# Fourth layer of a graph network: two edge tiles summed in one PSUM bank, and two of three pairs of tiles gathered plainly

## Chip, cores and metric

The kernel runs on one core of a Trainium2 chip. The metric is device time in microseconds (us) of one execution of the whole program, the median of several runs. Everything is one launch.

## What is computed

A node table x of 3125 rows and 256 columns goes through four graph layers, each followed by `x = layernorm(x + layer(x))`. There are 53125 edges with a source, a destination (sorted), 128 attributes and a type. Only the fourth layer matters here. It is a transformer convolution done twice (relu between), with 4 heads of 64 channels:

```
k_j   = k[src] + e                  # e = edge_attr @ We + be
alpha = einsum('ehc,ehc->eh', q[dst], k_j) / 8
ex    = exp(alpha - segment_max(alpha, dst)[dst])
msg   = (v[src] + e) * ex / segment_sum(ex, dst)[dst]
out   = segment_sum(msg, dst) + x @ Ws + bs
```

## The kernel before

Nodes stand in 25 blocks of 128 rows. The sorted edges are cut into tiles of 128 edges, each tile with destinations in one block only: 440 tiles (`ET`), about 17 or 18 to a block. The function `attend` runs one pass over all 440 tiles; it is called twice, for the two convolutions. Two neighbouring tiles are a pair (220 pairs, `PAIRS`), eight pairs a batch of 16 tiles (`NB`).

For each pair, the engines do this:

- GpSimd gathers, with one indirect DMA a tile, 128 rows of 516 floats (key, value and a column a head) by source from `kv_tab` into `t_kv`, a ring of 40 tiles (`UB`). There are two ways. An *accumulating* gather (L1850) adds the rows to what stands in the ring; ScalarE has first filled it with the edge terms (`fill`, L1962 and L1963). A *plain* gather (L1846) writes the rows, and VectorE adds the edge terms afterwards (`add_edge_terms`, L1872 and L1874). `plain(p)` says which pair is which: before, every second one.
- TensorE makes the edge terms (L2022), and picks the queries of the destinations with one-hot matrices (`queries`, L2034).
- VectorE multiplies keys and queries (L1884), sums over channels (L1890), takes its share in the running softmax of a batch (`sm.dve`), and weighs two of four heads of eight tiles at once (L1899); ScalarE weighs the other two (L2003) and makes one-hots of destinations (L1972, L1974).
- TensorE multiplies a tile's one-hots by its weighed rows (`scatter`, L2053): the tile's sums over destinations, 128 x 260, in one of three PSUM banks (`WIN3`). VectorE adds this window to the block's sums in `acc` in SBUF (`add_window`, L1921), at a block number held in a register (loaded eight at a time, L154).

The order is written out by hand as steps. In step p each engine treats pair p in its first half of the work and pair q = p - 11 (`LAG`) in its second: the sums of pair q are multiplied in TensorE's step p and added in VectorE's step p + 1. There is one semaphore `products` (TensorE's finished tiles), which frees one-hots, ring slots and lets VectorE add, and one `added` (VectorE's additions), which frees the banks. On entering a new batch, VectorE rescales a block's sums for the new maximum (`rescale`, L1912).

Ahead of the passes, `start_up` makes the tables from the sorted edges. All phases are separated by a barrier of all engines.

## Time and profile before

| | us |
|---|---|
| median of 3 runs | 4127.81 |
| lowest, highest | 4125.18, 4128.53 |
| span of the profiled execution, first to last instruction | 4145.4 |
| pass 1: first gather to last addition to the sums | 2475.8 to 3228.9 |
| pass 2: the same | 3348.0 to 4098.7 |

The profiled execution is not timed by itself beside its span; the three runs are executions of the same program without the profiler. PE is TensorE, PEld its weight loads, DVE VectorE, ACT ScalarE, POOL GpSimd, SP SyncE; a q behind a name is that engine's instruction queue. A row's duration includes its start and its drain, so two rows of one engine can overlap by some 80 ns: what an instruction costs its engine is read from start to next start.

### The profile page before, as it was taken

How to read it: one execution, taken by the hardware profiler on the slowest of the kernel's cores; microseconds unless marked ns; L12 is line 12 of the kernel's file. 1: busy time of each engine (PE TensorE's matmuls, PEld its weight loads, DVE VectorE, ACT ScalarE, POOL GpSimd, SP SyncE). 2: the span in 40 equal slices, each digit the busy share in tenths (PEclk: the TensorE clock that was granted, in tenths of full speed). 3: DMA queues.
4: the chain of work that ended last, by engine and by line, in shares of the span. 5: the costliest groups of instructions: out<-in, count | busy, mean ns of one | idle time of the engine just before them, and what ended most of it. 6: DMA issues, size and time to landing. Idle time of an engine off the chain costs nothing. (4 is left out here: it accounts for less than half of the span.)

```text
span 4145.4 us, 56575 instructions
## 1 busy us (share of the span) xinstructions
PE 2931.3 (71%) x12389; PEld 2013.0 (49%) x12389; DVE 2921.6 (70%) x6934; ACT 1927.7 (47%) x5796; POOL 2507.2 (60%) x2316
## 2 busy tenths in 40 slices
PE   4566566266777795467666587888888878888884
PEld 3444444144444463344444335666665446666662
DVE  3455555577777754355555648999999759999997
ACT  3444444211111133222223446878787348888884
POOL 5666664366666301666666048888886268888881
PEclk7667777578888896666767799999999999999997
DMA  5655444366666421344434249999997489999993
GB/s 158 136 135 132 133 135 105 121 187 202 200 201 193 154 92 53 106 114 114 113 111 110 41 151 225 223 219 223 219 224 180 139 200 223 226 222 226 225 222 104
DMA packets 363228, 673.24 MB, mean 162 GB/s; under 512 B 65028, under 2 KB 167413, under 8 KB 362910
## 3 DMA queue, kind: packets, MB, share of 16 engines
q0 software_dynamic: 160896, 403.63, 43.2%
q1 hardware_dynamic: 197902, 262.18, 19.4%
q10 hardware_dynamic: 4112, 3.83, 0.3%
q8 instruction: 123, 2.02, 0.2%
q14 instruction: 195, 1.60, 0.1%
HBM read 579.68 MB, written 89.74 MB: 161 GB/s over the span
## 5 line engine op out<-in xcount | busy, mean ns | idle before, releaser
L1850 POOL DMA_INDIRECT t_kv<-kv_tab,srcT x440 | 713.0, 1620 | 152.7 <-issue 130.7
L2053 PE MATMUL bank<-t_kv,t_oh 128*128 128x260 f32 x1760 | 519.8, 404 | 144.6 <-DVE acc L1921 68.3
L1410 POOL DMA_INDIRECT grow<-h_tab,srcT x440 | 417.1, 948 | 297.7 <-issue 98.1
L533 POOL DMA_INDIRECT grow<-h_tab,srcT x440 | 418.0, 950 | 251.6 <-issue 110.7
L878 POOL DMA_INDIRECT grow<-x_tab,srcU x416 | 394.3, 948 | 245.7 <-issue 109.4
L1846 POOL DMA_INDIRECT t_kv<-kv_tab,srcT x440 | 456.4, 1037 | 134.1 <-issue 123.1
L1013 PE MATMUL bank<-grow,oh 128*128 128x272 f32 x832 | 324.7, 497 | 195.1 <-DVE acc L931 107.8
L2022 PE MATMUL bank<-we,t_aT 128*128 128x256 f32 x1760 | 436.4, 388 | 24.1 <-DMA t_aT<-attrT_tab 21.0
L2003 ACT ACTIVATE t_kv<-t_kv 128x64 f32<-128x64 f32 x1696 | 445.2, 333 | 0.0
L2053 PEld LDWEIGHTS bank<-t_kv,t_oh 128*128 128x128 f32 x1760 | 284.8, 191 | 261.1 <-issue 150.5
L2034 PE MATMUL bank<-H,t_ohT 128*128 x2640 | 367.5, 276 | 18.8 <-DVE t_ks L1884 18.4
L608 DVE TENSOR_TENSOR acc<-acc,bank 128x258 f32 x440 | 186.7, 424 | 271.9 <-PE bank L704 120.1
L704 PE MATMUL bank<-grow,oh 128*128 128x258 f32 x880 | 334.6, 551 | 58.5 <-DVE acc L608 40.3
L1921 DVE TENSOR_TENSOR acc<-acc,bank 128x260 f32 x880 | 366.8, 417 | 11.5 <-PE bank L2053 6.6
L1526 PE MATMUL bank<-grow,oh 128*128 128x257 f32 x880 | 348.0, 539 | 29.2 <-DVE acc L1452 24.8
L2022 PEld LDWEIGHTS bank<-we,t_aT 128*128 128x128 f32 x1760 | 332.6, 195 | 74.0 <-DMA t_aT<-attrT_tab 22.6
L1452 DVE TENSOR_TENSOR acc<-acc,bank 128x257 f32 x440 | 185.2, 421 | 246.3 <-DMA atail<-in_edge_attr 118.4
L1884 DVE TENSOR_TENSOR t_ks<-t_kv,bank 128x512 f32<-128x512 f32 x440 | 299.7, 681 | 66.0 <-DMA t_kv<-kv_tab,srcT 56.6
L931 DVE SCALAR_TENSOR_TENSOR acc<-bank,in_first,acc 128x272 f32 x416 | 208.0, 500 | 188.7 <-PE bank L1013 72.9
L966 ACT COPY H<-bank 128x512 f32<-128x512 f32 x110 | 64.2, 586 | 556.4 <-PE bank L986 232.5
L1013 PEld LDWEIGHTS bank<-grow,oh 128*128 128x128 f32 x832 | 157.8, 227 | 314.3 <-issue 306.1
L2034 PEld LDWEIGHTS bank<-H,t_ohT 128*128 128x128 bf16 x2640 | 255.6, 99 | 104.3 <-issue 26.1
(406 smaller groups left out, 5611.5 us busy)
## 6 DMA issues: line engine op xcount, KB each, us to landing
t_aT<-attrT_tab SPq DMA_DIRECT2D x110, 512.0 KB
H<-in_edge_attr SPq DMA_DIRECT2D x440, 64.0 KB
attrT_tab<-H SPq DMA_DIRECT2D x55, 512.0 KB
t_ohT<-place_tab SPq DMA_DIRECT2D x110, 256.0 KB
H<-lo_tab SPq DMA_DIRECT2D x55, 256.0 KB
grow<-h_tab,srcT POOLq DMA_INDIRECT x880
place_tab<-H SPq DMA_DIRECT2D x55, 256.0 KB
wbig<-place_tab SPq DMA_DIRECT2D x55, 256.0 KB
```

What stands on the lines that cost most here:

```text
L533: nc.gpsimd.indirect_dma_start(out=grow[:, t % RA, :], out_offset=None, in_=h_tab, in_offset=bass.IndirectOffsetOnAxis(ap=srcT[:, t:t + 1] ...
L878: nc.gpsimd.indirect_dma_start(out=grow[:, t % RA, 0:F], out_offset=None, in_=x_tab, in_offset=bass.IndirectOffsetOnAxis(ap=srcU[:, t:t + ...
L1013: nc.tensor.matmul(PS[t % WIN1][:, 0:AC], oh[:, g % 2, u, :], grow[:, t % RA, :], start=True, stop=True).then_inc(products, 1)
L1410: nc.gpsimd.indirect_dma_start(out=grow[:, t % R2, :], out_offset=None, in_=h2_tab, in_offset=bass.IndirectOffsetOnAxis(ap=srcT[:, t:t + 1 ...
L1526: nc.tensor.matmul(PS[2 + t % WIN2][:, 0:F + 1], oh[:, t // HB % 2, t % HB, :], grow[:, t % R2, 0:F + 1], start=True, stop=True).then_inc( ...
L1846: nc.gpsimd.indirect_dma_start(out=kv[:, u, :], out_offset=None, in_=kv_tab, in_offset=row).then_inc(g_ready[u], 16)
L1850: nc.gpsimd.indirect_dma_start(out=kv[:, u, :], out_offset=None, in_=kv_tab, in_offset=row, compute_op=ALU.add).then_inc(g_ready[u], 16)
L1921: nc.vector.tensor_tensor(window, window, PS[4 + t % WIN3][:, 0:LHW], ALU.add).then_inc(added, 1)
L2003: last = nc.scalar.activation(part, part, ACT.Copy, scale=u_rows[:, t % UB, h, C3:C3 + 1])
L2022: mm = nc.tensor.matmul(PS[j % 2][:, v * F:(v + 1) * F], aT[:, g % 3, u * P:(u + 1) * P], we[:, :], start=True, stop=True)
L2034: mm = nc.tensor.matmul(PS[2 + p % 2][:, v * F:(v + 1) * F], ohT[:, g % 3, u * P:(u + 1) * P], Q3[:, ds(blocks[u], 1), n, :].rearrange("p ...
L2053: nc.tensor.matmul(PS[4 + t % WIN3][:, 0:LHW], oh[:, t % OHS, :], kv[:, t % UB, F:KVW], start=True, stop=True).then_inc(products, 1)
```

## The change

Tiles of a pair are now summed in PSUM where they belong to the same block. The one-hot product of pair r's first tile opens window r in a bank. The product of its second tile is made one pair later, after the first product of pair r + 1: it adds into window r if both tiles have the same block, and into window r + 1 if a new block begins with it. A number for each pair (`turn_i`, 0 or 1), made at start-up, says which; TensorE loads it into a register and takes the bank from it. This needs at least two tiles in each block, so the tile count of a block is raised to 2 where it is lower. The last pair of each batch can't share with the next batch, since the sums are rescaled between: its second tile has a window of its own. That makes 220 + 28 = 248 windows a pass, in the same three banks. `products` counts pairs now. VectorE adds windows one step later, the steps are one more, and the rescaling is one step later. Besides, two of three pairs are gathered plainly (146 plain pairs, 74 accumulating). The eight PSUM banks are declared as one tensor; two small tensors are given free earlier to make room.

```diff
+def last_of_batch(r):
+    return r % PB == PB - 1 or r == PAIRS - 1
+def window_no(r):
+    return r // PB * (PB + 1) + r % PB
...
+        def window_by_turn(first, r, turn, width):
+            here, there = r % PB % WINS, (r % PB + 1) % WINS
+            two = BANKS[:, first + here:first + there + 1, :] if here < there else BANKS[:, first:first + WINS, :][:, ::-2, :]
+            return two[:, ds(turn, 1), 0:width].rearrange("p a c -> p (a c)")
...
+                        step(nc.vector.tensor_scalar(n_b[:, 0:NT], n_b[:, 0:NT], 2.0, None, ALU.max))
...
+                        dve.wait_ge(starts_in, 32)
+                        nc.vector.tensor_tensor(turn_i[:, :], block_i[0:1, 1:ET:2], block_i[0:1, 0:ET:2], ALU.not_equal)
...
-        STEPS = PAIRS + LAG + 1
+        STEPS = PAIRS + LAG + 2
...
-            return p % 2 == 1
+            return p % 3 > 0
...
-                                    pool.wait_ge(products, t + 2 - UB)
+                                    pool.wait_ge(products, (t - UB) // 2 + 1)
...
-                            if 1 <= q:
-                                add_window(first, blocks[first % HB])
+                            if q >= 2 and q % 4 == 2:
+                                blocks = following
+                            if q >= 2 and not last_of_batch(q - 2):
+                                add_window(q - 2, blocks)
+                            elif q >= 2:
+                                add_own_window(q - 2, blocks)
                             if p < PAIRS:
                                 sum_channels(p)
-                            if 1 <= q:
-                                add_window(first + 1, blocks[(first + 1) % HB])
-                            if q >= 0 and q % 4 == 0 and q < PAIRS:
-                                blocks = following
+                            if q >= 1 and last_of_batch(q - 1):
+                                add_window(q - 1, blocks)
...
-                            if q >= 0 and q % 8 == 0 and q < PAIRS:
-                                sm.take_factor(dve, q // 8)
-                                rescale(q // 8, blocks[0])
+                            if q % PB == 0 and 0 <= q < PAIRS:
+                                sm.take_factor(dve, q // PB)
+                            if q % PB == 1 and 0 < q < PAIRS:
+                                rescale(q // PB, following[0])
...
-                                if t >= WIN3:
-                                    pe.wait_ge(added, t - WIN3 + 1)
-                                nc.tensor.matmul(PS[4 + t % WIN3][:, 0:LHW], oh[:, t % OHS, :],
-                                                 kv[:, t % UB, F:KVW], start=True, stop=True).then_inc(products, 1)
+                        def first(r):
+                            t, n = 2 * r, window_no(r)
...
+                            if n >= WINS:
+                                pe.wait_ge(added, n - WINS + 1)
+                            nc.tensor.matmul(window_of(4, r, LHW), oh[:, t % OHS, :], kv[:, t % UB, F:KVW], start=True, stop=True, skip_group_check=True)
+
+                        def second(r, turn):
+                            t, n = 2 * r + 1, window_no(r) + 1
...
+                            if last_of_batch(r):
+                                pe.wait_ge(added, n - WINS + 1)
+                                nc.tensor.matmul(own_window_of(4, r, LHW), ones_of, rows_of, start=True, stop=True, skip_group_check=True).then_inc(products, 1)
+                            else:
+                                nc.tensor.matmul(window_by_turn(4, r, turn, LHW), ones_of, rows_of, start=False, stop=True, skip_group_check=True).then_inc(products, 1)
...
                             if 0 <= q < PAIRS:
-                                scatter(q)
+                                first(q)
+                                if q % PB:
+                                    if q % 4 == 1:
+                                        turn = turns(q - 1, 4)
+                                    second(q - 1, turn[(q - 1) % 4])
+                                if last_of_batch(q):
+                                    second(q, None)
```

## Rows read from the trace of the kernel before

**Rows 1.** Cores: span and mean granted TensorE clock.

```profile
core 0: 4145.4 us, clock 0.841
```

**Rows 2.** Windows: length, busy us (instructions) of PE, PEld, DVE, ACT, POOL; clock, DMA share, GB/s.

```profile
2600.00:3150.00 550.00, 464.52 (x2531) 348.93 (x2531) 525.27 (x1153) 440.59 (x1399) 448.25 (x335) 1.00 0.96 222
3450.00:4000.00 550.00, 468.79 (x2559) 352.97 (x2558) 530.14 (x1161) 445.38 (x1415) 446.84 (x339) 1.00 0.96 223
1000.00:1150.00 150.00, 107.05 (x382) 65.43 (x381) 113.45 (x241) 17.86 (x33) 95.69 (x101) 0.90 0.65 200
```

**Rows 3.** Timeline of POOL, two pairs: start, us, instruction, idle before and its releaser.

```profile
2999.57 1.57 POOL L1850 DMA_INDIRECT t_kv<-kv_tab,srcT  x1 [0.30 <-issue]
...
3003.30 1.00 POOL L1846 DMA_INDIRECT t_kv<-kv_tab,srcT  x1 [0.31 <-issue]
...
3005.88 1.57 POOL L1850 DMA_INDIRECT t_kv<-kv_tab,srcT  x1 [0.30 <-issue]
```

**Rows 4.** Single lines in pass 1 (four rows), pass 2: ns min/median/max, first to last start.

```profile
L1850 POOL DMA_INDIRECT t_kv<-kv_tab,srcT x220: 1552/1571/2591, 2475.8 to 3192.6; - x110
L1846 POOL DMA_INDIRECT t_kv<-kv_tab,srcT x220: 962/997/1996, 2479.5 to 3195.8; - x110
L1884 DVE TENSOR_TENSOR t_ks<-t_kv,bank x220: 668/681/690, 2483.2 to 3203.1; 128x512 f32<-128x512 f32 x110
L1921 DVE TENSOR_TENSOR acc<-acc,bank x440: 390/418/427, 2523.0 to 3228.5; 128x260 f32 x147
L1850 POOL DMA_INDIRECT t_kv<-kv_tab,srcT x220: 1557/1566/2582, 3348.0 to 4059.8; - x110
L1846 POOL DMA_INDIRECT t_kv<-kv_tab,srcT x220: 959/997/1962, 3351.7 to 4062.9; - x110
```

**Rows 5.** Timeline of POOL, a long gather.

```profile
2808.70 2.38 POOL L1850 DMA_INDIRECT t_kv<-kv_tab,srcT  x1 [0.30 <-issue]
```

**Rows 6.** Timeline of DVE around it.

```profile
2807.16 0.42 DVE L1921 TENSOR_TENSOR acc<-acc,bank 128x260 f32 x1
2807.49 0.68 DVE L1890 TENSOR_REDUCE t1s_al<-t_ks 128x8 f32<-128x512 f32 x1
...
2808.42 1.22 DVE L1899 TENSOR_TENSOR t_kv<-t_kv 128x1024 f32<-128x1024 f32 x1
2809.56 0.68 DVE L1872 TENSOR_TENSOR t_kv<-t_kv,bank 128x512 f32<-128x512 f32 x1
2810.16 0.68 DVE L1874 TENSOR_TENSOR t_kv<-t_kv,bank 128x512 f32<-128x512 f32 x1
```

**Rows 7.** Waits of DVE, 2600 to 3150: us in total, times, longest us.

```profile
DVE t_ks L1884 <- DMA t_kv<-kv_tab,srcT: 7.2, 6, 2.9
DVE t_kv L1872 <- DMA t_kv<-kv_tab,srcT: 5.5, 12, 0.8
DVE t_ks L1884 <- issue: 3.1, 4, 1.3
```

**Rows 8.** Line L154, 2600 to 3150: register loads on TensorE's queue, ns min/median/max.

```profile
L154 PEldq TENSOR_LOAD <-block_i x42: 587/592/1297, 2609.3 to 3149.3; - x42
```

**Rows 9.** Waits of PE, 2600 to 3150, the largest.

```profile
PE bank L2053 <- DVE acc L1921: 23.4, 35, 1.5
```

**Rows 10.** DMA, 2600 to 3150: packets, MB; and by queue, with share of 16 engines.

```profile
DMA packets 49635, 122.05 MB, mean 222 GB/s; under 512 B 6697, under 2 KB 6697, under 8 KB 49574
...
q0 software_dynamic: 37531, 88.52, 78.3%
```

**Rows 11.** Timeline of the tail of pass 1, DVE and then ACT.

```profile
3218.34 0.43 DVE L1921 TENSOR_TENSOR acc<-acc,bank 128x260 f32 x1 [0.21 <-PE bank L2053]
3218.98 0.43 DVE L1921 TENSOR_TENSOR acc<-acc,bank 128x260 f32 x1 [0.21 <-PE bank L2053]
...
3217.56 0.68 ACT L1972 ACTIVATE t_oh<-iota_n,dlocT 128x128 f32<-128x128 f32 x2
...
3218.69 0.68 ACT L1972 ACTIVATE t_oh<-iota_n,dlocT 128x128 f32<-128x128 f32 x2
```

More of the change, by code:

```diff
@@ L45 @@
 KVW = 256 + LHW
+PAIRS = ET // 2
+PB = NB // 2
+WINS = 3
 BIG = 1.0e30
@@ L50, with pairs_behind @@
 NREL = 16
+def last_of_batch(r):
+    return r % PB == PB - 1 or r == PAIRS - 1
+def window_no(r):
+    return r // PB * (PB + 1) + r % PB
+def pairs_behind(t):
+    return t // 2 if t % 2 == 0 and t // 2 % PB else t // 2 + 1
 class Chain:
@@ L131, in graph_layers, with window_of, own_window_of @@
         we = sb("we", [ED, F])
-        PS = [ctx.enter_context(nc.psum_tensor(f"bank{i}", [P, 512], F32)) for i in range(8)]
+        BANKS = ctx.enter_context(nc.psum_tensor("bank", [P, 8, 512], F32))
+        PS = [BANKS[:, i, :] for i in range(8)]
         accf = acc[:, :, :].rearrange("p a b -> p (a b)")
+        def window_of(first, r, width):
+            return BANKS[:, first + r % PB % WINS, 0:width]
+        def own_window_of(first, r, width):
+            return BANKS[:, first + (r % PB + 1) % WINS, 0:width]
+        def window_by_turn(first, r, turn, width):
+            here, there = r % PB % WINS, (r % PB + 1) % WINS
+            two = BANKS[:, first + here:first + there + 1, :] if here < there else BANKS[:, first:first + WINS, :][:, ::-2, :]
+            return two[:, ds(turn, 1), 0:width].rearrange("p a c -> p (a c)")
         def ds(start, n):
@@ L163, in graph_layers @@
         start_i = held(first_layers, "start_i", [1, EA], I32)
+        first0 = held(first_layers, "first0", [1, NBT])
+        iota_r = held(first_layers, "iota_r", [P, NREL])
         s_tab = held(first_layers, "s_tab", [P, NT, 2])
@@ L1909, in rescale, with add_to, add_window, add_own_window @@
                             if c > 0:
-                                dve.wait_ge(added, c * NB)
+                                dve.wait_ge(added, c * (PB + 1))
                             part = acc[:, ds(block_of_first, 1), 0:LHW].rearrange("p a (h c) -> p (a h) c", h=H3)
                             nc.vector.tensor_tensor(part, part, sm.fm[:, :].unsqueeze(2).broadcast_to([P, H3, C3 + 1]), ALU.mult).then_inc(sm.rescaled, 1)
-                        def add_window(t, block_of):
-                            dve.wait_ge(products, t + 1)
-                            if t > 0:
-                                dve.wait_ge(added, t)
-                            if t % NB == 0:
-                                dve.wait_ge(sm.rescaled, t // NB + 1)
-                            window = acc[:, ds(block_of, 1), 0:LHW].rearrange("p a c -> p (a c)")
-                            nc.vector.tensor_tensor(window, window, PS[4 + t % WIN3][:, 0:LHW], ALU.add).then_inc(added, 1)
+                        def add_to(block_of, bank, number):
+                            if number > 0:
+                                dve.wait_ge(added, number)
+                            window = acc[:, ds(block_of, 1), 0:LHW].rearrange("p a c -> p (a c)")
+                            nc.vector.tensor_tensor(window, window, bank, ALU.add).then_inc(added, 1)
+                        def add_window(r, blocks):
+                            dve.wait_ge(products, r + 1)
+                            if r % PB == 0:
+                                dve.wait_ge(sm.rescaled, r // PB + 1)
+                            add_to(blocks[2 * r % HB], window_of(4, r, LHW), window_no(r))
+                        def add_own_window(r, blocks):
+                            dve.wait_ge(products, r + 1)
+                            add_to(blocks[2 * r % HB + 1], own_window_of(4, r, LHW), window_no(r) + 1)
                         nc.vector.memset(u_rows[:, :, :, C3:C3 + 1], 0.0).then_inc(zeroed, 1)
@@ L1928, in _ @@
                             q, batch = p - LAG, softmax_at(p)
-                            first = 2 * q - 2
                             if p < PAIRS:
@@ L1960, in fill @@
                             if 2 * p >= UB:
-                                act.wait_ge(products, 2 * p + 2 - UB)
+                                act.wait_ge(products, p + 1 - UB // 2)
                             nc.scalar.copy(kv[:, u:u + 2, 0:F], e)
@@ L1968, in one_hots @@
                             if 2 * q >= OHS:
-                                act.wait_ge(products, 2 * q + 2 - OHS)
+                                act.wait_ge(products, q + 1 - OHS // 2)
                             pair = oh[:, 2 * q % OHS:2 * q % OHS + 2, :]
```

28 lines of the change are left out of this document (14 added, 14 removed).

## The prediction

> **What bounds the kernel now.** I read the stages first: in both passes of the fourth layer VectorE is busy 95 to 96% of the time, the 16 DMA engines 96%, TensorE 84 to 85% at its upper clock, GpSimd 81 to 82% [rows 2]. Four nearly full resources; which one sets the pace must come from the order of time. GpSimd issues its gathers in a cycle of two pairs: 3.73 us for the two accumulating gathers of one pair (2999.57 to 3003.30) and 2.58 us for the two plain ones of the next (3003.30 to 3005.88), and the 0.30 us ahead of each gather has no releaser but "issue" [rows 3]. So the missing 18% is the engine's own gap: GpSimd waits for nobody. A pass has 110 pairs of each kind: 110 x 6.31 = 694.1 us. From the first gather to the end of the last it takes 721.0 us (2475.8 to 3195.8 + 1.0) in pass 1 and 715.9 us in pass 2 [rows 4]. The rest, 26.9 and 21.8 us, is in gathers that take longer than their kind: the one at 2808.70 took 2.38 us for 1.57 [rows 5], and VectorE's weighing (L1899) had begun at 2808.42 [rows 6].
>
> VectorE trails right behind. Its last product with the queries starts at 3203.1, 6.3 us after GpSimd's last gather of pass 1 has ended [rows 4], and nearly all its waits in a 550 us stretch are for gathers: 7.2 + 5.5 + 3.1 = 15.8 us [rows 7]. GpSimd's 335 gathers there are 167.5 pairs, so a step lasts 550 / 167.5 = 3.28 us, and without those waits VectorE would need (550 - 15.8) / 167.5 = 3.19 us. GpSimd is the bound, VectorE 3% behind it. The kernel's end is not of interest: what a pass saves moves all that follows, since each phase ends in a barrier.
>
> **The change part by part, each pass.**
>
> *Plain gathers, 146 pairs instead of 110 (p % 3 > 0), accumulating ones 74.* GpSimd: 74 x 3.73 + 146 x 2.58 = 652.7 us for 694.1, that is 41.4 less. The long gathers stay: the weighing comes as often as before. With the mean rest of 24.3 us GpSimd needs 677.0 us, 3.077 a pair. This is a bound from below on the pass unless that rest shrinks too; at best, with no rest at all, 24 us more would go.
>
> VectorE has to add the edge terms of 36 more pairs, two additions of 128x512 each, 0.60 us apart from start to start (2809.56 to 2810.16) [rows 6]: 36 x 2 x 0.60 = +43.2 us. ScalarE loses 36 pairs of two copies; it is not the bound (80% busy [rows 2]), so I count nothing.
>
> These new additions could slow GpSimd as the weighing does. The long gather of [rows 5] overlaps L1899, whose three operands all lie in SBUF; the gathers around the additions L1872 and L1874, which read one operand from a bank of PSUM, are of normal length [rows 3, 6]. By this trace they cost GpSimd nothing; if they cost it as much as L1899 does (about 0.8 us a time), 36 x 2 x 0.8 = 58 us would eat the gain, which I hold unlikely, since 110 pairs of them are in the 694 us already. [...]
>
> *Sums in PSUM: 248 additions for 440.* An addition of 260 columns (L1921) takes 0.33 us from its start to that of the next instruction (2807.16 to 2807.49) [rows 6]. 192 x 0.33 = -63.4 us. VectorE together: -63.4 + 43.2 = -20.2 us, 0.092 a pair: 3.19 - 0.09 = 3.097 us a pair, 681 us a pass. That is 0.02 above GpSimd's 3.077: the two are level.
>
> TensorE makes the same products; the second tile of a pair adds into a bank at an address taken from a register. It also loads four such numbers once in four pairs. The load of eight numbers takes 0.59 us on its queue [rows 8], and I take this as the price of four too; the lower bound is nothing (hidden while the array works off the queue), the upper 55 x 0.59 = 32 us a pass on TensorE. What hides it is TensorE's idle time, 550 - 464.5 = 85.5 us in 167.5 pairs [rows 2], 0.51 us a pair. At a step of 3.1 us this falls to 0.33, and 0.15 of it goes to the load at worst. So I count nothing, with the cover thin.
>
> *The ring of three banks.* Before, TensorE's second product of a pair waits for the addition that VectorE makes in the same step; this is its largest wait, 23.4 us in 35 times [rows 9], and VectorE hardly ever waited for TensorE in turn [rows 7]. Now, inside a batch of eight pairs, the first product of pair q needs the window of pair q-3, which VectorE added one step ago: the wait goes. At a batch's end two products (the last pair's own window, and the first window of the next batch) still need the same step's addition. What is queued behind them is the next step's edge terms and queries, up to 2.4 us, for which VectorE comes after the rest of its step and the whole next one, over 4 us. I count nothing. The rows of a pair are given free, and its sum is added, one step later; a gather of pair p needs pair p-20, finished eight steps earlier instead of nine, far ahead.
>
> *DMA.* The engines are 96% busy at 222 GB/s here [rows 2]. In a stage of plain gathers alone they move 200 GB/s at 65% [rows 2], so a plain byte costs 0.65/200 against 0.96/222, three quarters. A pair moves 0.73 MB (122.05 MB, of which the gathers are 88.52, in 167.5 pairs [rows 10]); at the plain price that is 2.37 us, the mean is 3.15, so an accumulating pair costs 3.93. After: (3.93 + 2 x 2.37) / 3 = 2.89 us a pair, under the other two. This is an estimate, as the other stage moves other rows too.
>
> *Head, tail and start-up.* In the tail the additions come 0.64 us apart, each waiting for the product and the product for a bank (1.28 a pair), while ScalarE's one-hots come every 1.13 us [rows 11]. With one addition a pair, the one-hots set the pace for about ten pairs: -1.5 us. One more step: +0.5. Start-up has one more link and one side instruction, 0.2 us in all.
>
> **The sum.** If VectorE and GpSimd need 3.097 and 3.077 us, the step is neither: each has its own bursts (softmax parts in three of eight steps, long gathers once in four pairs), and neither has slack to repair them. Before, with 3% between the two, VectorE ended 6.3 us behind; with none, it will fall further back. I take 3.11 a pair, between 3.10 and the 3.14 that keeping half of the present waits (0.05) would give. 220 x 3.11 = 684.2 for a mean of 718.4: -34.2, with the tail -35.2 a pass, two passes -70.4, start-up +0.2: **-70 us**. The profiled span is 4145.4 us [rows 1], 17.6 above the median of the timed runs; the difference is in what lies around them, and I take the saving as the same in both: span 4075, median 4127.8 - 70 = **4058 us**.
>
> **Rivals.**
> *TensorE comes late.* It loses 0.33 us of idle time to the shorter step and to the load, and its order is rigid. For: it is 84% busy. Against: VectorE waits for it almost never now, and the wait for the addition goes. If half the load shows up, with stalls to match, the step is 3.16 (695 us, -24 a pass with the tail): 4080; at 3.20 (704 us, -15 a pass): 4097.
> *The DMA engines were the bound and a plain gather saves them nothing.* Then the step can't go below 0.96 x 3.28 = 3.15 us: 693 us a pass, -54 in all: 4074. Against: the stage of plain gathers, and GpSimd's cycle without a gap.
> *GpSimd's rest shrinks too*, as VectorE crosses it less often: a fifth to a third of 24.3 us goes, and VectorE keeps up: -46 a pass with the tail, -92: 4036.
> *Nothing comes of it* (VectorE is the true bound and its saving is used up by new waits): within 8 us of 4128.
> *Slower: the batch ends.* TensorE stands at the last pair's own window until VectorE's addition of the same step, then at the next batch's first window again. VectorE's cover is over 4 us against 2.8 us of work (0.4 for the product, 2.4 for edge terms and queries). It decides where each batch end is late beyond that cover by more than 70 / 55 = 1.3 us (55 batch ends in two passes); at 1.7 us it is 94 - 70 = +24: 4152. What speaks for it is only that both waits are new in place.
>
> **Chances.** My forecast 0.52; TensorE late 0.22; DMA 0.08; rest shrinks 0.06; nothing 0.05; slower 0.07. Range: 4038 (forecast with the tail and half the rest) to 4100 (TensorE late, weak end); it leaves out nothing, slower and some of the best case. The forecast's own range is 4045 to 4070. Within 0.2% of the time before (8 us) this kernel's runs can't be told from no change: faster 0.88, same 0.05, slower 0.07.
>
> **What would show it.** GpSimd in a cycle of three pairs, 3.73 + 2 x 2.58 = 8.9 us, and near 680 us from first to last gather. VectorE over 97% busy, its waits for gathers under half, 248 rows of the addition a pass with 292 edge-term additions. TensorE's wait for the addition at batch ends alone. DMA share near 0.92. I am wrong if GpSimd shows waits for ScalarE's fills or for products (then something behind it holds it), or if VectorE waits for TensorE's queries or products for more than 5 us a pass.

## The result, and the profile after

The changed kernel takes 4163.66 us (median of 4 runs, 4157.72 to 4176.26) where the kernel before takes 4128.17 us beside it: ratio 1.0085, 95% interval 1.0071 to 1.0099. It is 0.85% slower; the prediction was 4058 us, 1.7% faster. The range of 4038 to 4100 us misses it by 64 us.

The cores, and then the windows of both passes, with the columns of [rows 1] and [rows 2]:

```profile
core 0: 4162.5 us, clock 0.821
```

```profile
2600.00:3150.00 550.00, 479.24 (x2475) 370.44 (x2475) 501.79 (x1039) 401.19 (x1313) 393.55 (x327) 0.93 0.85 216
3450.00:4000.00 550.00, 474.01 (x2458) 367.84 (x2457) 499.37 (x1030) 400.91 (x1310) 394.80 (x328) 0.93 0.85 216
```

VectorE falls from 95.5% to 91.2%, the DMA share from 0.96 to 0.85, and GpSimd makes 327 gathers for 335 [rows 2]. TensorE alone is busier (479.2 for 464.5 us, in fewer pairs: 479.24 / 163.5 = 2.93 us a pair for 464.52 / 167.5 = 2.77) and its granted clock falls from 1.00 to 0.93 on average: parts of the passes run at the lower of its two levels, 1.2 GHz. Where all but one engine have more room and the pass gets longer, they wait for one another.

The instructions themselves are as predicted. Single lines of pass 1 (columns of [rows 4]):

```profile
L1886 POOL DMA_INDIRECT t_kv<-kv_tab,srcT x292: 942/963/1971, 2461.7 to 3183.3; - x146
L1890 POOL DMA_INDIRECT t_kv<-kv_tab,srcT x148: 1547/1564/1835, 2457.9 to 3186.5; - x148
```

292 plain gathers and 148 accumulating ones, with nearly the durations of before (963 ns in the middle for 997, 1564 for 1571); yet from first to last they take 3186.5 + 1.6 - 2457.9 = 730 us where 721 was needed before. The waits between 2600 and 3150 us (engine and line, what it waited for, us in total, times, longest):

```profile
POOL t_kv L1890 <- ACT t_kv L2012: 63.6, 27, 3.9
...
ACT t_kv L2011 <- PE bank L2071: 52.6, 21, 5.6
...
PE bank L1368 <- DVE t1s_al L1930: 14.9, 11, 1.6
...
PE bank L1372 <- DVE t1s_run L1392: 11.7, 7, 3.1
PE bank L2101 <- DVE acc L1958: 11.1, 6, 1.8
...
DVE t1s_d L1416 <- PE bank L1378: 6.8, 6, 1.6
DVE t1s_top L1409 <- PE bank L1375: 5.2, 9, 1.0
DVE t1s_run L1392 <- PE bank L1369: 4.8, 7, 0.7
...
DVE t1s_tiles L1396 <- PE bank L1372: 4.1, 7, 0.6
```

GpSimd, which had hardly waited for anybody, now stands 63.6 us for ScalarE's fills (L2012), ScalarE 52.6 us for TensorE's edge terms (L2071), and VectorE's waits for gathers [rows 7] have been replaced by waits for TensorE inside the running softmax (L1392 to L1416). Those four rows add to 20.9 us. Other rows name a transfer or nothing where the same instruction waits for the same product (L1392 <- DMA skip_tab: 6.9 us). Both of the prediction's "I am wrong if" conditions hold.

Where it happens is seen in a timeline of the second step of a batch (start, us, instruction, idle before and its releaser):

```profile
2818.30 0.26 PE L1375 MATMUL bank<-ident,t1s_into 1*128 1x1 f32 x1
...
2818.49 2.54 PE L2071 MATMUL bank<-we,t_aT 128*128 128x256 f32 x8
2818.60 0.35 DVE L1409 SCALAR_TENSOR_TENSOR t1s_top<-pen_row,bank,t1s_run 64x128 f32<-64x128 bf16 x1 [0.71 <-issue]
2818.96 0.36 DVE L1410 SCALAR_TENSOR_TENSOR t1s_top<-pen_row,bank,t1s_run 64x128 f32<-64x128 bf16 x1
...
2820.20 0.59 ACT L2011 COPY t_kv<-bank 128x512 f32<-128x512 f32 x1 [2.73 <-PE bank L2071]
...
2820.86 0.82 PE L2083 MATMUL bank<-H,t_ohT 128*128 x6
...
2821.52 0.27 PE L1378 MATMUL bank<-ident,t1s_top 128*128 128x128 f32 x1
...
2821.54 1.57 POOL L1890 DMA_INDIRECT t_kv<-kv_tab,srcT  x1 [1.40 <-ACT t_kv L2012]
...
2821.83 0.29 DVE L1416 TENSOR_REDUCE t1s_d<-bank 128x64 f32<-128x128 f32 x1 [1.45 <-PE bank L1378]
```

VectorE's L1410 ends at 2819.32 and has given TensorE the input of its next softmax product, L1378. TensorE comes to it at 2821.52: in the order written out for it stand eight rows of L2071, the edge terms of two pairs, and the queries (L2083). VectorE waits 1.45 us for the answer. ScalarE waits 2.73 us for the first pair's half of the same eight rows, and GpSimd 1.40 us for ScalarE. The clock has a part in this: the eight rows take 2.54 us here, and 1.89 us where the clock is at its upper level (the timeline of x_three below, at a granted clock of 1.00). The windows row of the stretch in which they start, with a granted clock of 0.53:

```profile
2816.00:2819.20 3.20, 3.20 (x11) 1.99 (x10) 2.40 (x10) 0.20 (x1) 2.29 (x4) 0.53 0.96 200
```

In the kernel before, p % 2 == 1 put the edge terms of two pairs into every even step and none into any odd one, so the product of a batch's second step never had any ahead of it. With p % 3 > 0 they come as two, one, none in a period that runs across the batches of eight.

I time a step as the interval between starts of L1924 (L1884 before), VectorE's product of keys and queries, over pairs 24 to 207 of both passes: mean 3.27 us before, 3.37 after, 3.11 forecast. By place in 24 pairs, the batches' first two steps take 5.80 + 4.42, 2.93 + 6.02 and 5.19 + 3.39 us, 9.25 on average, where they took 4.60 + 3.17 = 7.77 before. The longest single step, 6.02, is the one with two pairs' edge terms ahead of L1378. The longest two together are not these but 5.80 + 4.42, with two pairs' edge terms in the first step and one pair's in the second.

### The profile page after: what moved, and what is told of

Same layout as the page of the kernel before. It is cut to its first block and busy times, and to the rows that moved or that the text cites. A ratio compares the mean times of both kernels' runs of the same rounds, so it can differ in the third digit from the quotient of the medians.

```text
span 4162.5 us, 55555 instructions
## 1 busy us (share of the span) xinstructions
PE 2971.9 (71%) x12389; PEld 2072.6 (50%) x12389; DVE 2887.2 (69%) x6696; ACT 1852.7 (45%) x5652; POOL 2398.0 (58%) x2316
## 5 line engine op out<-in xcount | busy, mean ns | idle before, releaser
L1886 POOL DMA_INDIRECT t_kv<-kv_tab,srcT x584 | 595.3, 1019 | 178.0 <-issue 166.1
L1890 POOL DMA_INDIRECT t_kv<-kv_tab,srcT x296 | 464.4, 1569 | 242.8 <-ACT t_kv L2012 166.9
L2071 PE MATMUL bank<-we,t_aT 128*128 128x256 f32 x1760 | 483.4, 413 | 20.8 <-DMA t_aT<-attrT_tab 20.7
L2083 PE MATMUL bank<-H,t_ohT 128*128 x2640 | 389.1, 285 | 24.0 <-DVE t_ks L1924 20.9
L2071 PEld LDWEIGHTS bank<-we,t_aT 128*128 128x128 f32 x1760 | 355.2, 208 | 78.9 <-DMA t_aT<-attrT_tab 22.3
L2101 PE MATMUL bank<-t_kv,t_oh 128*128 128x260 f32 x880 | 294.5, 418 | 65.5 <-DVE acc L1958 32.1
L2083 PEld LDWEIGHTS bank<-H,t_ohT 128*128 128x128 bf16 x2640 | 266.8, 102 | 129.2 <-issue 44.0
L1924 DVE TENSOR_TENSOR t_ks<-t_kv,bank 128x512 f32<-128x512 f32 x440 | 299.1, 680 | 38.5 <-DMA t_kv<-kv_tab,srcT 31.9
L1055 PEld LDWEIGHTS bank<-grow,oh 128*128 128x128 f32 x832 | 157.6, 227 | 312.6 <-issue 305.0
L746 PEld LDWEIGHTS bank<-grow,oh 128*128 128x128 f32 x880 | 234.1, 279 | 137.3 <-ACT grow L721 49.0
L2021 ACT ACTIVATE t_oh<-iota_n,dlocT 128x128 f32<-128x128 f32 x880 | 301.4, 391 | 1.7 <-PE bank L2112 1.5
```

What stands on the lines that cost most here:

```text
L746: nc.tensor.matmul(PS[t % WIN][:, 0:F + 2], oh[:, g % 2, u, :], grow[:, t % RA, :], start=True, stop=True).then_inc(products, 1)
L1055: nc.tensor.matmul(PS[t % WIN1][:, 0:AC], oh[:, g % 2, u, :], grow[:, t % RA, :], start=True, stop=True).then_inc(products, 1)
L1886: nc.gpsimd.indirect_dma_start(out=kv[:, u, :], out_offset=None, in_=kv_tab, in_offset=row).then_inc(g_ready[u], 16)
L1890: nc.gpsimd.indirect_dma_start(out=kv[:, u, :], out_offset=None, in_=kv_tab, in_offset=row, compute_op=ALU.add).then_inc(g_ready[u], 16)
L2021: last = nc.scalar.activation(pair[:, v, :], iota_n[:, :], ACT.Abs, bias=dlocT[:, 2 * q + v:2 * q + v + 1], scale=-1.0)
L2071: mm = nc.tensor.matmul(PS[j % 2][:, v * F:(v + 1) * F], aT[:, g % 3, u * P:(u + 1) * P], we[:, :], start=True, stop=True)
```

## The experiments

Each is timed beside the kernel before (4130.6 to 4134.9 us in these jobs), so ratios are compared. The short diffs are against the changed kernel unless the text says otherwise.

### One part of the change at a time

x_sums keeps every second pair plain and has only the sums in PSUM; x_plain is the kernel before with two of three pairs plain.

```
-            return p % 3 > 0
+            return p % 2 == 1        # x_sums
```

```
-            return p % 2 == 1        # x_plain, in the kernel before
+            return p % 3 > 0
```

> The sums in PSUM alone: every second pair gathered plainly, as before. If the gather pattern is what costs (it no longer falls on the same pairs of each batch), this one stays at GpSimd's pace of before, 716 to 721 us a pass, and is within 5 us of before (4128), with the clock at its upper level in the passes. If the sums in PSUM or the new order of TensorE's products cost, it is as slow as the changed kernel or slower (over 4150), with a fall of the granted clock in each batch.

> Two of three pairs gathered plainly alone, windows as before, 440 additions. VectorE then has 43 us more a pass than before: without new stalls (3.19 + 0.20 = 3.39 us a step) 745 us a pass, the kernel near 4128 + 2 x 27 = 4180. If the pattern also disturbs the batch starts, by about 2 us a batch as in the changed kernel, it is near 4250. Under the theory that the sums in PSUM are the cause of the disturbance, the batch starts are undisturbed and the clock stays up.

x_sums: 4123.94 us, ratio 0.9987 (0.9975 to 0.9999). x_plain: 4221.86 us, 1.0228 (1.0210 to 1.0247). The windows of x_sums and two of its waits:

```profile
2600.00:3150.00 550.00, 465.19 (x2527) 357.75 (x2526) 477.31 (x999) 438.26 (x1397) 448.53 (x334) 0.98 0.96 222
```

```profile
DVE t_ks L1924 <- DMA t_kv<-kv_tab,srcT: 41.8, 25, 2.9
...
PE bank L2101 <- DVE acc L1958: 5.0, 13, 0.7
```

The sums free VectorE (477 us busy for 525) and TensorE's wait for the addition falls from 23.4 us [rows 9] to 5.0, as predicted; GpSimd keeps its pace, so VectorE waits for gathers instead and the time stays. So VectorE was not the bound; GpSimd, whose rows show no wait, fits as the one that was. The whole loss comes with the new pattern of gathers: it makes GpSimd's instructions cheaper, and the pass gets longer.

x_plain is slower for another reason too. Its windows, and GpSimd's wait for the fills:

```profile
2600.00:3150.00 550.00, 453.73 (x2402) 343.12 (x2400) 529.57 (x1144) 392.18 (x1276) 378.94 (x318) 0.97 0.84 211
```

```profile
POOL t_kv L1850 <- ACT t_kv L1963: 85.4, 41, 5.1
```

VectorE, with all 440 additions and the new edge terms, is busy 96.3% of the time, 529.57 / 159 = 3.33 us a pair for 3.14 before. It is held mostly by VectorE's own work, and GpSimd stands for the fills all the same: that wait alone doesn't tell which engine is late.

### Order, and the clock

x_order moves the softmax product L1372 of a batch's first step behind that step's edge terms and queries, so that TensorE doesn't stand at it. x_warm puts four products of constants ahead of L1368 and of L1372, to hold the clock at its upper level.

```
-                            if batch and batch[1] == 0:
-                                sm.pe(pe, batch[0], 1, sums_done, 0)
...
                                 queries(p + 1, blocks)
-                            if batch and batch[1] > 0:
+                            if batch:
```

```
+                            if batch and batch[1] == 0 and 0 <= q < PAIRS:
+                                warm(q, 4)          # 4 times ones x ident into the window's bank that the step opens
```

> The changed kernel with the transpose of the running maxima (second softmax part of a batch) moved behind the next pair's edge terms and queries on TensorE. If the loss is that TensorE stands at this transpose in the batch's first step while the queries of the next pair are queued behind it, 1 to 1.7 us a batch come back: 4163 - 55 x 1 to 1.7 = 4070 to 4110. If the loss is elsewhere (the first softmax product, the clock), it is within 10 us of 4163 or slower, since VectorE's second part then waits for the later transpose.

> The changed kernel with four products of two constant tiles (sent to the window that TensorE opens next, overwritten by it) ahead of each of the first two softmax products of a batch, in the time in which TensorE stands. If the half clock of about 3.4 us after these waits is what makes TensorE late, the falls go and 1 to 2 us a batch come back: 4060 to 4110. If the clock is only a companion of the wait, the falls may go and the time stays within 10 us of 4163, or rises by the products' own time (up to 55 x 1.7 = 94).

x_order: 4186.13 us, 1.0161 (1.0120 to 1.0203), worse than the changed kernel. The wait moves: VectorE's L1396 waits 12.8 us (5 times) for L1372, where it had waited 4.1. So it doesn't help to let TensorE pass by L1372. x_warm: 4186.50 us, 1.0149 (1.0126 to 1.0172). Its profiled execution is the fastest of the four, 4163.4 us, the changed kernel's time, and has the clock nearly restored:

```profile
2600.00:3150.00 550.00, 493.57 (x2811) 395.86 (x2810) 499.17 (x1041) 400.81 (x1313) 392.06 (x328) 0.98 0.85 217
```

```profile
DVE t1s_run L1392 <- DMA skip_tab<-skip: 14.4, 6, 2.5
...
DVE t1s_d L1416 <- PE bank L1378: 1.7, 3, 0.7
```

0.98 for 0.93, and VectorE does no more pairs in the window (499.2 us busy for 501.8). The Trainium skill, "TensorE: Matmul & The Clock Gate", section "HAM oscillation — how this bites in real kernels", puts the price of such oscillation at half of the time at the low level. With 0.93, 14% of the window is at the low level, and my estimate by that page is up to 7%; TensorE's own busy time agrees (2.93 us a pair for 2.77, 6% more). Whether the kernel's time pays it x_warm can't tell, since its products cost time too. The wait for L1378 falls from 6.8 to 1.7 us, and the step of 6.02 us to 4.70: a part of that lateness is the clock's. But the added products stand ahead of L1368 and L1372, and VectorE's wait at L1392 for L1368's sum grows (the first row; 6.9 us in the changed kernel). What one place gives, the other takes, and the clock's share in the loss isn't separated.

### Other patterns of plain pairs

Three of these gather 5 of 8 pairs plainly, in a period of one batch. x_misfit adds on the way in pairs 1, 4 and 7 of every eight, x_fit in 2, 4 and 5, x_fit_alone does as x_fit in the kernel before (single sums). x_late keeps p % 3 and makes the filled pair's edge terms of each batch's second step behind the softmax product.

```
-            return p % 3 > 0
+            return p > 0 and p % 8 not in (1, 4, 7)     # x_misfit; (2, 4, 5) in x_fit and x_fit_alone
```

```
-                            if p + AHEAD + 1 < PAIRS and not plain(p + AHEAD + 1):
+                            if p + AHEAD + 1 < PAIRS and not plain(p + AHEAD + 1) and not late(p):   # late: p % 8 == 1
...
                                 sm.pe(pe, batch[0], 2 * batch[1] + 1, sums_done, 0)
+                            if p + AHEAD + 1 < PAIRS and not plain(p + AHEAD + 1) and late(p):
+                                edge_terms(p + AHEAD + 1)
```

> The changed kernel with a gather pattern of period eight, as long as a batch: pairs 2, 4 and 5 of eight accumulating (and pair 0 of the pass), the others plain. TensorE then has one pair's edge terms in the first step of a batch and none in the second, where two softmax products have to come in time. If the place of the edge terms in a batch is the cause, the batch starts lose nothing: GpSimd needs (3 x 3.73 + 5 x 2.58) / 8 + 0.11 = 3.12 us a pair, VectorE 3.05, so 3.12 to 3.16 a step and 4128 - 2 x 24 to 33 = 4062 to 4080. If more plain pairs disturb wherever they are, or the clock falls in any case, it is above 4130.

> The same numbers of accumulating and plain gathers as in the run with pairs 2, 4 and 5, but accumulating are pairs 1, 4 and 7 of eight: TensorE has the edge terms of two pairs in the second step of every batch. If their place is the cause, each batch loses about 2 us: 55 x 2 = 110 above the other, 4170 to 4190. If the place is of no account, the two are equal within 10 us.

> The changed kernel (two of three plain), but in the second step of a batch TensorE makes the edge terms for the accumulating pair behind the softmax product of that step and not ahead of it. This touches one batch in three. If that product's lateness is the cause there, 1 to 2 us come back in 18 batches: 4164 - 18 to 36 = 4128 to 4146. If not, no change (4155 to 4172), or slower, since ScalarE's filling and GpSimd's gather come later.

> The kernel before with the pattern of pairs 2, 4 and 5, and no sums in PSUM: VectorE has 440 additions and 27 more plain pairs, 3.19 + 0.15 = 3.34 us a step, 735 a pass: 4128 + 2 x 16 = 4160. If it is at or below 4128, the sums in PSUM are not needed for the gain.

x_misfit: 4159.65 us, 1.0063 (1.0040 to 1.0085). It puts two pairs' edge terms into the second step of every batch, and that step takes 6.38 us in all of them, after a first step of 2.98. Its VectorE waits:

```profile
DVE t1s_d L1416 <- DMA h_tab<-lasts_f: 24.9, 9, 3.4
DVE t1s_d L1416 <- PE bank L1378: 12.6, 10, 2.0
```

Both rows are the wait for L1378 (a semaphore of TensorE's; the transfer named in the first happened to end last): 37.5 us for 6.8 in the changed kernel. So a wait at the second step can be made by placing edge terms there. The time doesn't follow it: the first two steps take 9.37 us in x_misfit and 6.98 in x_fit (below), and x_misfit is the faster by 62 us. It was expected 110 us slower, so the theory that the place of the edge terms at the batch starts decides the time fails here.

x_late shortens the worst second step from 6.02 to 5.29 us, and takes 4184.32 us, 1.0130 (1.0103 to 1.0157): new waits of VectorE come three and four steps later (steps 12 and 13 of 24 take 4.14 and 4.21 us for 3.08 and 2.72; 12.6 us in 15 times at L1929, its product with the queries). What was taken out of one place is lost in others.

x_fit: 4221.32 us, 1.0209 (1.0168 to 1.0250), and x_fit_alone 4228.24, 1.0235 (1.0204 to 1.0266). The batches' first three steps are level as I wanted (4.20, 2.78, 3.99 us), but the other steps take more: the fourth 4.18 us (2.21 in x_misfit) with a stall of another kind, the sixth 3.82 (2.73). Both are far above what was expected, 4062 to 4080 and 4160 us. Timeline of x_fit:

```profile
2813.54 0.60 PE L2112 MATMUL bank<-t_kv,t_oh 128*128 128x260 f32 x2
...
2814.41 0.82 PE L2083 MATMUL bank<-H,t_ohT 128*128 x6
...
2815.36 0.68 DVE L1924 TENSOR_TENSOR t_ks<-t_kv,bank 128x512 f32<-128x512 f32 x1
...
2819.13 0.42 DVE L1958 TENSOR_TENSOR acc<-acc,bank 128x260 f32 x1 [3.09 <-DMA tail_tab<-atail]
...
2819.70 0.77 PE L2101 MATMUL bank<-t_kv,t_oh 128*128 128x260 f32 x1 [4.46 <-issue]
```

VectorE waits 3.09 us for a product that, by its row, ended at 2814.14, and TensorE is idle for 4.46 us, waiting in turn for the addition. (The transfer named as releaser is chance; L1958 has no wait on one.)

### Is TensorE's signal late?

x_push and x_fit_push put one small product of constants behind the queries and one behind the window's products, so that no signalling product is the last before TensorE stands. In both, the small product starts a group of its own in the bank of an unfinished sum, which loses the first tile's part; the results are not the kernel's. (The Trainium skill, "PSUM — Partial Sum Buffer", section "The four PSUM rules", has this: a first product clears a whole bank's state.) The instructions are the same.

```
                                 queries(p + 1, blocks)
+                                push(q - 1)
...
                                     second(q, None)
+                                push(q)         # ones x ident, 64 columns, into the open window's bank
```

> The changed kernel, with one small product of constants (64 columns, in columns of a window's bank that nobody reads) behind the queries and one behind the window's products of every step; its results are used by nobody. Theory A: the signal that TensorE gives with its last product before it stands waiting comes late (in the kernel with pairs 2, 4 and 5 added on the way, VectorE and ScalarE went on 3 to 5 us after TensorE's last recorded row), and VectorE's waits at the batch starts come from it; another product behind it brings the signal at once. Then VectorE's gaps fall from 48 us towards the 25 us of the kernel before and the time is 4070 to 4130 us. Theory B: TensorE simply reaches the softmax products late, in its written order, and signals are on time. Then the small products only add some 0.3 us of work to TensorE's step, and the time is 4160 to 4210 us.

> The same two small products a step in the kernel whose pairs 2, 4 and 5 of every eight are added on the way (4221 us, 29 stalls of 2.6 us on average at the fourth step of a batch, each with TensorE idle 4 to 5 us between the queries and the next window's product). Theory A (late signal): the stalls of the fourth step vanish, 75 us less, 4130 to 4160 us. Theory B: TensorE and VectorE stand waiting for something that the trace names wrongly, and the stalls stay: 4215 to 4260 us.

x_push: 4227.97 us, 1.0243 (1.0213 to 1.0274); x_fit_push: 4308.00 us, 1.0416 (1.0382 to 1.0450), both above even what theory B gave. The stalls of the fourth step stay (some 66 us in 24 times over pairs 24 to 207). So a later product does not bring the signal. Theory A falls, and what holds the product of x_fit stays open. What the pair does show is how dear TensorE's time is: the 768 small products, mostly two a step, add 64 us to the changed kernel.

### Less work for TensorE

x_light has one product of three for the queries and half the columns of the edge terms; its results are not the kernel's. Waits, order and all other engines are as in the changed kernel. x_light_before is the same cut in the kernel before.

```
-                                mm = nc.tensor.matmul(PS[j % 2][:, v * F:(v + 1) * F], aT[...], we[:, :], ...)
+                                mm = nc.tensor.matmul(PS[j % 2][:, v * F:v * F + F // 2], aT[...], we[:, 0:F // 2], ...)
...
-                                for n in range(3):
+                                for n in range(1):
```

> The changed kernel with less work on TensorE: one product of three for the queries and half the columns of each edge term, all else (waits, other engines, gathers) as it is; some 0.9 us less of TensorE's 2.9 us a step. Theory T: TensorE's own work in front of the softmax products makes it late, and that is what the batch starts lose. Then VectorE's gaps fall towards those of the kernel before and the time comes to GpSimd's or VectorE's own, 4050 to 4100 us. Theory R: the round trips between VectorE and TensorE and their order set it, whatever lies in front. Then the time stays within 4140 to 4170 us.

> The kernel before with the same lighter work on TensorE, as the control. GpSimd never waits there, so both theories say the same: 4120 to 4135 us. Should it fall well below that, TensorE costs the kernel before something too, through the speed of GpSimd's gathers.

x_light: 4082.52 us, 0.9883 (0.9867 to 0.9900). x_light_before: 4128.89 us, 0.9990 (0.9979 to 1.0001). The windows, x_light and then x_light_before:

```profile
2600.00:3150.00 550.00, 404.93 (x1926) 299.77 (x1925) 527.61 (x1093) 427.78 (x1402) 420.92 (x346) 0.87 0.90 227
```

```profile
2600.00:3150.00 550.00, 402.00 (x1892) 289.85 (x1890) 531.60 (x1169) 445.56 (x1420) 446.66 (x340) 0.87 0.97 225
```

Waits of x_light:

```profile
POOL t_kv L1890 <- ACT t_kv L2012: 28.8, 18, 2.6
...
DVE t1s_d L1416 <- PE bank L1378: 4.5, 7, 0.9
...
DVE t1s_top L1409 <- PE bank L1375: 1.3, 5, 0.4
```

This is the run that decides. The same cut of TensorE's work is worth nothing before and 81 us after. VectorE is 95.9% busy again, its step 3.19 us, although the clock averages 0.87. The gain is where theory T puts it: the first two steps of a batch together take 7.86 us for 9.25 in the changed kernel (7.77 before), the other six 17.64 for 17.71. Theory T holds, R falls: what the plain gathers met is TensorE's own time, which the kernel before could hide. The run cuts the edge terms and the queries alike, so it doesn't say that the place of the edge terms alone is at fault; and it doesn't part VectorE's waits for the softmax products from GpSimd's for the fills, which shrink together.

### Spreading TensorE's work

x_even sets AHEAD (how many pairs ahead the edge terms for ScalarE's fills are made) to 6 in the changed kernel, which puts one pair's edge terms into every step of TensorE. x_three is the changed kernel with pairs 2, 4 and 6 of eight added on the way; x_three_even has AHEAD 6 as well. x_three_behind is x_three with the filled pairs' edge terms behind the queries.

```
-        AHEAD = 5
+        AHEAD = 6                                      # x_even, x_three_even
```

```
-            return p % 3 > 0
+            return p > 0 and p % 8 not in (2, 4, 6)    # x_three, x_three_even, x_three_behind
```

```
-                            if p + AHEAD + 1 < PAIRS and not plain(p + AHEAD + 1):     # x_three_behind
-                                edge_terms(p + AHEAD + 1)
...
                                 queries(p + 1, blocks)
+                            if p + AHEAD + 1 < PAIRS and not plain(p + AHEAD + 1):
+                                edge_terms(p + AHEAD + 1)
```

> The changed kernel with AHEAD 6 in place of 5: the edge terms that ScalarE fills in are made one step earlier, so that TensorE makes the edge terms of one pair in every step, in place of two, one and none in turn. Theory T: the steps that make two pairs' edge terms are the ones in which TensorE is late for VectorE; one a step removes that, 4070 to 4130 us. Theory R, or a ring of 40 gathered tiles that is now one pair shorter of slack: 4150 to 4200 us, with GpSimd waiting for the fills or ScalarE for the products.

> The changed kernel, with pairs 2, 4 and 6 of every eight added on the way (5 of 8 gathered plainly, as in the kernel with 2, 4 and 5). GpSimd alone would need 718.4 - (1/8)/(1/6) x 41.4 = 687 us a pass, 62 us less for both: 4062 us beside 4124 for the sums alone. Theory C: a batch's steps stay level only while edge terms never come in two steps running; here TensorE makes them in steps 0, 2, 4, 6 and 7, so the early steps of a batch are those of the kernel before, and the time is 4060 to 4110 us. Rival D: any departure from every second pair costs more than it gives, as the three others did (4160 to 4221): 4140 to 4220 us, and then VectorE waits at the step whose edge terms moved.

> The kernel with pairs 2, 4 and 6 of every eight added on the way (4117 us), with AHEAD 6 too: TensorE then makes the edge terms of one pair in steps 0, 2, 3, 4, 5 and 6, of two in step 7 and of none in step 1, in place of two in steps 0, 4 and 6. Theory T: its stall at the sixth step (33 times 1.4 us in 46 batches, VectorE waiting for the window's product of the step before) vanishes, and the time is 4070 to 4105 us. Rival: the slack of the ring is what is short, and the time is 4115 to 4150 us.

> Pairs 2, 4 and 6 of every eight added on the way (4117 us), and TensorE makes the edge terms that ScalarE fills in behind the queries in place of ahead of VectorE's edge terms. Theory T: no step of TensorE then has two pairs' edge terms in one run, a product is followed by at most one pair's, and VectorE's wait at the sixth step shrinks from 1.4 us a time to under 0.5: 4095 to 4112 us. Rival: the fills come later by what was put ahead of them (1.7 us), GpSimd waits for them and the next first product is late by as much: 4120 to 4150 us.

x_even: 4140.94 us, 1.0026 (1.0011 to 1.0041), between both ranges. By the ratios some 24 us of a loss of 35 come back with the bunching of edge terms gone (the second step of 6.02 us falls to 4.44, the first two steps together from 9.25 to 8.34), and 11 stay.

x_three: **4117.14 us, 0.9966 (0.9954 to 0.9978)**, faster than both kernels, and just above the expected 4060 to 4110. Its edge terms come in steps 0, 2, 4, 6 and 7 of a batch, so that steps 1 and 3 have none, as in the kernel before (step 2 has one pair's for two), and the first two steps take 6.87 us. It gains only 7 to 9 us on x_sums, where GpSimd's cheaper gathers were to give 62. GpSimd hardly waits for fills; what is left is a stall at the sixth step:

```profile
DVE acc L1958 <- PE bank L2112: 18.9, 14, 2.0
...
POOL t_kv L1890 <- ACT t_kv L2012: 7.8, 3, 2.8
```

```profile
2696.54 0.60 PE L2112 MATMUL bank<-t_kv,t_oh 128*128 128x260 f32 x2
...
2696.98 1.89 PE L2071 MATMUL bank<-we,t_aT 128*128 128x256 f32 x8
...
2698.48 0.43 DVE L1958 TENSOR_TENSOR acc<-acc,bank 128x260 f32 x1 [2.04 <-PE bank L2112]
```

x_three_even: 4155.36 us, 1.0059 (1.0038 to 1.0079), and x_three_behind: 4221.68 us, 1.0211 (1.0193 to 1.0230), against theory T both, and above their rivals' ranges too. Waits of x_three_behind, from the slowest of its five executions (4247.0 us), the one that was profiled:

```profile
ACT t_kv L2011 <- PE bank L2071: 116.8, 47, 4.1
...
PE bank L2101 <- ACT t_oh L2023: 64.6, 27, 4.2
...
POOL t_kv L1890 <- ACT t_kv L2012: 54.9, 40, 2.7
DVE acc L1958 <- PE bank L2112: 32.5, 26, 3.0
```

The rows fit one ring of waits: ScalarE stands at a fill (L2011) for TensorE's edge terms and so is late with the one-hots (L2023) that TensorE needs for L2101; TensorE is late with the products that VectorE adds, and GpSimd stands at the fill. Moving an edge term earlier (x_three_even) or later (x_three_behind) costs 38 and some 100 us over x_three.

## Why the prediction was wrong, step by step

**What bounds the kernel before: right.** x_sums frees VectorE of 48 us in 550 and gains 0.13%; x_light_before frees TensorE, and its ratio of 0.9990 can't be told from no change. GpSimd waited 1.2 us for fills in 550, and what it costs per pair set the pace. The DMA engines, at 0.96 in both runs, are kept apart from it only by GpSimd's rows without waits.

**GpSimd's 41.4 us a pass: right in kind, too small.** The gathers' rows of pass 1 add to 529.5 us for 587.3 before, 57.8 less: besides the cheaper kind, a plain gather takes 963 ns for 997 in the middle, and fewer gathers are long. That is the "rest" that the forecast kept at 24.3 us. In x_light pass 1 still takes 692 us from first gather to the end of the last, against the forecast bound of 677, because GpSimd stands for fills. In the changed kernel GpSimd's own work no longer counts: it waits 63.6 us in 550.

**No slowing by the new edge-term additions: right.** In the kernel before, 78 of 880 gathers are over 0.15 us longer than their kind, and all of them overlap L1899; none of the 236 that overlap L1872 or L1874 without it is. The rows that the prediction names for it show this only in part, since [rows 3] and [rows 6] are of different stretches.

**VectorE's sum: right.** After, 501.79 us in 163.5 pairs are 3.07 us a pair of busy time, x_light has 527.61 / 173 = 3.05; before it was 525.27 / 167.5 = 3.14. The saving is 0.07 to 0.09 us for the forecast 0.092.

**DMA: right.** 0.85 x 550 / 163.5 = 2.86 us a pair for the forecast 2.89, and 3.15 before. The DMA rival took a plain gather to save these engines nothing; it saves them.

**The ring of banks: right in kind.** In x_sums TensorE's wait for the addition falls from 23.4 to 5.0 us. The slower rival, two waits at a batch's end, is not what happened: the wait for the addition fell in the changed kernel too, to 11.1 us, all six times at the first window of a new batch.

**The step that failed: TensorE, "So I count nothing, with the cover thin".** I divided TensorE's idle time by the pairs, found 0.51 us a pair falling to 0.33, and took that mean as cover for whatever comes. But TensorE runs one written order, and at the start of a batch VectorE asks it for a product and waits for the answer several times in two steps. Each of those answers is late by what stands ahead of it. With p % 2 the product L1378 of the second step had no edge terms ahead of it; with p % 3 it has eight rows, four or none (2818.49 to 2821.52 in the timeline). I counted the 36 more pairs of edge terms on VectorE and never looked at where the edge terms fall on TensorE. The size: x_light takes 81 of the 105.7 us between forecast and result. In steps, 3.37 - 3.19 = 0.18 us of the 0.26 by which 3.11 was missed; 440 steps of 0.18 are 79 us. That TensorE's time at the batch starts is the cause is shown by x_light and its control. That the place of the edge terms makes it so is shown for single steps only: x_misfit and x_fit moved the waits as expected and the time the other way. The step also took TensorE's busy time as given; it rose from 2.77 to 2.93 us a pair with the clock at 0.93, and no run says how much of the 81 us that is.

The register load, the only cost that this step did price, was no part of it: x_sums has it and loses nothing, and in the changed kernel four values take 335 ns, not 0.59 us:

```profile
L191 PEldq TENSOR_LOAD <-turn_i x41: 331/335/1028, 2601.3 to 3139.9; - x41
```

The rival "TensorE comes late" named the engine and its rigid order, but priced it as half of a register load with stalls, 4080 to 4097.

**ScalarE, "it is not the bound (80% busy [rows 2]), so I count nothing": failed too, as a link.** A fill that waits for TensorE's edge terms holds GpSimd's next accumulating gather, and ScalarE's one-hots behind it. In the kernel before GpSimd stood 1.2 us for fills in the same stretch, for 63.6 now.

**The step taken as 3.11: 0.08 too low even with light TensorE** (3.19). VectorE's idle time is still 0.13 us a step there, about half of it in the same softmax waits, with GpSimd standing 28.8 us for fills. I took two coupled, nearly level engines as losing 0.01 to 0.02. (The lower end of the range, the forecast with half the rest, comes to 4058 - 24 = 4034 and not 4038.) The remainder, 24 us between x_light and the forecast, is measured but its cause isn't separated.

**Left open.** Why, in x_fit, VectorE and ScalarE go on only 4 to 5 us after the product's row has ended, with TensorE idle; and in x_three 1.3 us after it, with eight rows running behind. It isn't that a signal waits for a later product (x_fit_push). Whether the product itself ended later than its row says, I can't tell: the ends are modelled. Nor do I know why patterns 2, 4, 5 and 2, 4, 6 differ by 104 us. TensorE makes the edge terms of 1, 0, 1, 0, 1, 1, 2, 2 pairs in the eight steps of a batch in the first and of 2, 0, 1, 0, 2, 0, 2, 1 in the second, so the slower has less ahead of it in the first steps.

## What to carry to other kernels

Idle time of an engine that runs a written order is not a pool. Before counting a shorter step as hidden by it, lay the new order beside the chain of questions and answers between two engines and see what stands ahead of each answer, over the least common period of the two patterns (three and eight here, 24). This finds where waits will come, not what the kernel will take: of the three patterns with a batch's period in the changed kernel, all 5 plain pairs in 8, one gained 0.34% and the others lost 0.63% and 2.1%. The cheapest test of such cover is a kernel in which one engine does less of the same, with the same cut in the kernel before as control: it told in one pair of runs what the moves of the order could not.

## What the runs showed of the hardware

- A lower mean clock needn't cost: 0.87 in the window of both kernels with the cut in TensorE's work, at 4082.52 and 4128.89 us. Where an answer of TensorE is awaited it can: the wait for L1378 fell from 6.8 to 1.7 us with the clock at 0.98 for 0.93 (x_warm), though the products that held the clock cost as much elsewhere.
- Small products are dear where TensorE is questioned often: 64 us for 768 of 64 columns in x_push, 0.08 us each; TensorE's busy time rose to 489.43 / 156 = 3.14 us a pair, from 2.93.
- The gap between a product's row and the start of what waits for it is not constant: in x_three 1.34 us (2696.54 + 0.60 to 2698.48) with eight rows behind it, in x_fit 5.0 us (2814.14 to 2819.13) with an idle TensorE.
